# Attention and mixture block on one Trainium2 core: own PSUM banks for logits, maxima and job pieces, and a new order of TensorE's step

## The reference, cut to what matters

```python
h = _layernorm(x) * (1 + ca) + sa
# 16 heads of 16, causal, softmax over the keys with its exact maximum
logits = einsum('bhqd,bhkd->bhqk', q, k) / sqrt(16)
attn = softmax(where(causal, logits, -inf))
x = x + ga * (attn_times_v(attn, v) @ W_out.T + b_out)
h = _layernorm(x) * (1 + cb) + sb
# a layer: base product plus three low-rank experts of rank 8, mixed by softmax gates per token
h = relu(mole(h, W1, b1, A1, B1, R1))          # 256 -> 1024
x = x + gb * mole(h, W2, b2, A2, B2, R2)       # 1024 -> 256
```

## Time and profile before

| what | value |
|---|---|
| median of three runs | 1724.15 us |
| the profiled execution | 1730.61 us |
| its span (first to last instruction) | 1728.9 us |
| first exponential starts | 125.39 us |
| end of the last attention step, about | 1616 us |
| TensorE busy | 1412.8 us (82%) |
| DVE, ACT, POOL busy | 961.8, 685.5, 561.6 us |
| mean granted clock of TensorE | 0.808 |

### The profile page before, as it was taken

One profiled execution on the slowest core, in us unless ns is written; L12 is line 12 of the kernel. 1 busy time (PEld: TensorE's weight loads), 2 busy tenths in 40 slices (PEclk: granted clock), 3 DMA queues, 4 the chain that ended last, 5 costly groups with the idle time before them and its releaser, 6 DMA issues. The chain is left out here.

```text
span 1728.9 us, 26273 instructions
## 1 busy us (share of the span) xinstructions
PE 1412.8 (82%) x10096; PEld 796.4 (46%) x10096; DVE 961.8 (56%) x1878; ACT 685.5 (40%) x935; POOL 561.6 (32%) x680
## 2 busy tenths in 40 slices
PE   4458898897998989899857988889888889899445
PEld 4334454544544434454423554536453445454245
DVE  6146566566576676763336556665756667761212
ACT  1113354353443445355522433344533444546210
POOL 5460151324440124332302341234432233233262
PEclk8666588788996888888965786888995899899758
DMA  5242223121321121220241223113121112100000
GB/s 149 77 133 79 74 81 101 34 64 31 99 71 49 38 55 57 67 77 20 80 114 47 75 87 83 34 37 104 51 75 40 48 30 71 50 10 13 31 18 13
DMA packets 83638, 106.68 MB, mean 62 GB/s; under 512 B 9002, under 2 KB 57074, under 8 KB 83516
## 3 DMA queue, kind: packets, MB, share of 16 engines
q1 hardware_dynamic: 83516, 105.01, 21.5%
HBM read 66.71 MB, written 37.75 MB: 60 GB/s over the span
## 5 line engine op out<-in xcount | busy, mean ns | idle before, releaser
L853 DVE TENSOR_REDUCE mx<-ps 128x1 f32<-128x512 f32 (+3 forms) x1152 | 706.8, 655 | 436.7 <-PE ps L570 241.0
L759 ACT ACTIVATE prob<-ps 128x1024 f32<-128x1024 f32 (+3 forms) x640 | 567.1, 896 | 700.1 <-PE ps L548 368.6
L570 PE MATMUL ps<-kst,qst 48*128 48x512 f32 (+3 forms) x1280 | 321.7, 497 | 135.5 <-DVE mx L853 108.5
L607 PE MATMUL ps<-prob,vw 128*17 128x512 f32 (+3 forms) x2560 | 353.3, 630 | 1.6 <-ACT o_sb L766 0.9
L543 PE MATMUL ps<-qst,kst 50*128 50x512 f32 (+3 forms) x1280 | 333.4, 519 | 8.3 <-ACT prob L759 5.6
L543 PEld LDWEIGHTS ps<-qst,kst 50*128 50x128 f32 x1280 | 138.7, 213 | 331.7 <-issue 146.2
L570 PEld LDWEIGHTS ps<-kst,qst 48*128 48x128 f32 x1280 | 155.2, 226 | 213.6 <-issue 158.4
L1030 POOL CAST hid_hi<-hidf 128x512 fp32r<-128x512 f32 x64 | 39.1, 612 | 341.7 <-ACT hidf L810 341.6
L578 PE MATMUL ps<-mask_q,pick 64*128 64x128 bf16 x1024 | 88.6, 255 | 0.0
L707 PE MATMUL ps<-w_hi,hid_hi 128*128 128x284 f32 x256 | 81.5, 339 | 8.2 <-POOL hid_lo L1031 8.1
L607 PEld LDWEIGHTS ps<-prob,vw 128*17 128x17 f32 x2560 | 44.3, 99 | 88.8 <-issue 62.9
(11 more groups left out here) (147 smaller groups left out, 1801.5 us busy)
## 6 DMA issues: line engine op xcount, KB each, us to landing
kst<-k_rows SPq DMA_DIRECT2D x160, 192.0 KB, 4.0
qst<-q_rows SPq DMA_DIRECT2D x64, 192.0 KB, 3.9
q_rows<-s_hi SPq DMA_DIRECT2D x64, 128.0 KB
k_rows<-s_hi SPq DMA_DIRECT2D x64, 128.0 KB
o_rows<-o_sb SPq DMA_DIRECT2D x32, 256.0 KB, 2.0
sx<-in_x SPq DMA_DIRECT2D x16, 256.0 KB, 2.9
q_rows<-sf SPq DMA_DIRECT2D x32, 128.0 KB
k_rows<-sf SPq DMA_DIRECT2D x32, 128.0 KB
```

The lines of the kernel that those rows point to most:

```text
L570: last = pe.matmul(ps[:, M_BANK + banks[a], at:at + width], qst[half, u % Q_BUFS, p, i * P:(i + 1) * P], kst[half, K_SLOT[u, c], p, 0:widt ...
L607: last = pe.matmul(ps[32 * h:32 * h + HD + 1, O_BANK, skip:BLK], vw[:, (NJ * b + t // 4) % V_BUFS, t % 4, g * GH + h, :], prob[:, s % P_BU ...
L759: act.activation(prob[:, s % P_BUFS, 2 * p:2 * p + 2, 0:width], ps[:, bank:bank + 2, 0:width], ACT.Exp).then_inc(a_free, 1)
L853: dve.tensor_reduce(mx[:, u % 2, a, both, i, c], ps[:, M_BANK + bank, 0:n * width].rearrange("p (h x) -> p h x", h=n), AX, ALU.max).then_i ...
```

## The change

What it does, part by part:

- **Banks.** Logits get three single banks (0 to 2) in turn, one per head. Maxima and turned maxima get three banks (3 to 5). All job pieces share the single bank 6, in the order of the steps (`J_ORDER`; semaphores j_full, j_free). Bank 7 stays.
- **Exponentials** are taken per head (128 x 512): 1280 instructions instead of 640. A logits pair waits for the exponentials up to the first head of the pair before it.
- **TensorE's step** becomes `values(s - 2)`, `logits(s, 0)`, turn, first maxima, job piece, `logits(s, 1)`, second maxima.
- **Drains a step later.** ACT empties the job piece of step s in step s + 1, between the exponentials of heads 1 and 2; DVE does so between its two maxima groups; POOL at the start of step s + 1.
- **`place()`** hangs the pieces on steps, with at most one piece's matmuls in a step. In steps 0 to 319 there are 213 pieces on 239 steps (f_down takes two). Before, 159 steps hold one piece, 38 two, 3 three, and 120 none; now 81 hold none. 169 pieces are followed by another piece in the very next step: 109 of the earlier ones are drained by ACT, 60 by DVE.
- **Ends.** The token blocks sx are double-buffered (two loads up front); the first four S blocks and the last two F blocks have the norm and the splits on DVE instead of POOL; the weight split moves from POOL at step -8 to ACT and DVE at step -20; S blocks are stored in two halves, each after its own split.
- **Denominators** are inverted once per chunk (d_load, one reciprocal of 128 x 64, d_store), and the inverse is loaded by four DMAs with the attention output; before, each F block loaded them by six and DVE inverted 128 x 512 numbers (L908). fx has three buffers instead of two.

The diff, cut to its core:

```diff
-A_SLOTS, M_BANK, M_BANKS, O_BANK = 2, 4, 3, 7
+A_BANKS, M_BANK, M_BANKS, J_BANK, O_BANK = 3, 3, 3, 6, 7
...
+def place():
+    when, taken = {}, set()
+    for chain, starts in ((S_CHAIN, S_START), (D_CHAIN, D_START), (F_CHAIN, F_START)):
+        for n, start in enumerate(starts):
+            s = start
+            for piece, gap in chain:
+                s += gap
...
+                width = WIDTH.get(piece, 0)
+                while any(s + d in taken for d in range(width)):
+                    s += 1
+                when[piece, n] = s
+                taken.update(range(s, s + width))
+                s += max(0, width - 1)
...
 def logits(s, p):
-                    if event >= A_SLOTS:
-                        pe.wait_ge(a_free, event - A_SLOTS + 1)
+                    if event >= A_BANKS - 1:
+                        pe.wait_ge(a_free, event + 2 - A_BANKS)
...
+                def job_bank(piece, n):
+                    if J_AT[piece, n]:
+                        pe.wait_ge(j_free, J_AT[piece, n])
...
 TensorE's loop
                     first, second = groups(s)
+                    if 0 <= s - PV_LAG < NSTEP:
+                        values(s - PV_LAG)
                     if 0 <= s < NSTEP:
                         logits(s, 0)
                     if s in TURN_AT:
                         turn_maxima(TURN_AT[s])
                     for u, k in first:
                         maximum(u, k)
-                    if 0 <= s - PV_LAG < NSTEP:
-                        values(s - PV_LAG)
+                    for piece, n in JOBS[s]:
+                        if piece in pieces:
+                            pieces[piece](n)
                     if 0 <= s < NSTEP:
                         logits(s, 1)
                     for u, k in second:
                         maximum(u, k)
-                    for piece, n in JOBS[s]:
-                        if piece in pieces:
-                            pieces[piece](n)
...
 ACT's loop
                         exponential(s, 0)
                         exponential(s, 1)
+                    for piece, n in JOBS[s - 1]:
+                        if piece in drains:
+                            drains[piece](n)
+                    if 0 <= s < NSTEP:
+                        exponential(s, 2)
+                        exponential(s, 3)
...
 DVE's loop
-                    for u, k in first + second:
+                    for u, k in first:
                         maximum(u, k)
+                    for piece, n in JOBS[s - 1]:
+                        if piece in drains:
+                            drains[piece](n)
+                    for u, k in second:
+                        maximum(u, k)
```

More of the change, by code:

```diff
@@ L44 @@
 ST_ROWS = ROWS + 2
[L45 removed]
+K_BUFS, Q_BUFS, V_BUFS, P_BUFS, FX_BUFS = 7, 3, 6, 3, 3
 PV_LAG = 2
@@ L71, in job_steps @@
+WHEN = place()
+BEGIN, END = min(S_START) - 1, max(WHEN.values()) + 3
+def job_steps():
+    at = {s: [] for s in range(BEGIN - 1, END + 1)}
+    for (piece, n), s in WHEN.items():
+        if WIDTH.get(piece, 0) == 2:
+            at[s].append((piece + "a", n))
+            at[s + 1].append((piece + "b", n))
+        else:
+            at[s].append((piece, n))
     return at
 JOBS = job_steps()
+J_ORDER = sorted((s, piece, n) for (piece, n), s in WHEN.items() if piece in WIDTH)
+J_AT = {(piece, n): k for k, (_, piece, n) in enumerate(J_ORDER)}
@@ L91, in pair_steps @@
 def pair_steps():
-    at = {s: [] for s in range(BEGIN - 5, END)}
+    at = {s: [] for s in range(BEGIN - 1, END)}
     for u in range(NU):
@@ L132, in rings @@
             take(("max", u, k, 1))
-        if 0 <= s < NSTEP:
-            a_at["exp", s, 1] = len(a_at)
-        for piece, n in JOBS[s]:
[L136 to L146, removed]
+    return at
+M_AT = maxima_banks()
 def key_loads():
     blocks = [(u, c) for u, (_, J, _) in enumerate(UNITS) for c in range(J + 1)]
-    at = {s: [] for s in range(BEGIN - 5, END)}
+    at = {s: [] for s in range(BEGIN - 1, END)}
     for kb, (u, c) in enumerate(blocks):
@@ L436, in batch, with standardise, two_parts @@
             return n * TB // S
+        def standardise(eng, link, dst, src, mv, tmp, ready):
+            for t in range(TT):
+                last = eng.tensor_scalar(dst[:, t], src[:, t], mv[:, t, 0:1], tmp[:, 1, t:t + 1],
+                                         ALU.subtract, ALU.mult)
+                if t < TT - 1:
+                    link(last, wait=False)
+            last.then_inc(ready, 1)
+        def two_parts(eng, link, parts, src, ready):
+            link(eng.tensor_copy(parts[0], src))
+            eng.tensor_tensor(parts[1], src, parts[0].bitcast(F32), ALU.subtract).then_inc(ready, 1)
         with nc.Block() as block:
@@ L542, in logits @@
                         half = slice(64 * a, 64 * a + ST_ROWS)
-                        last = pe.matmul(ps[:, bank + a, 0:width], kst[half, slot, p, t % 4 * P:(t % 4 + 1) * P],
+                        last = pe.matmul(ps[:, banks[a], 0:width], kst[half, slot, p, t % 4 * P:(t % 4 + 1) * P],
                                          qst[half, u % Q_BUFS, p, skip:BLK], start=True, stop=(t < 4 * J))
@@ L547, in logits @@
                             half = slice(64 * a, 64 * a + 64)
-                            last = pe.matmul(ps[:, bank + a, 0:P], pick[half, w - a + 1], mask_k[half, w - a + 1],
+                            last = pe.matmul(ps[:, banks[a], 0:P], pick[half, w - a + 1], mask_k[half, w - a + 1],
                                              start=False, stop=(w == 1))
```

510 lines of the change are left out of this document (268 added, 242 removed).

## The result

The changed kernel takes 2053.32 us (median of four runs, 2043.85 to 2057.45); the kernel before, run beside it, 1728.22 us. The ratio is 1.188, 95% interval 1.180 to 1.196: slower by 19%. The prediction had the direction and the wait for the bank, but said 1831 us, in a range that ended at 1925.

The account below looks back on a forecast made before the run. The prediction took TensorE's own work to bound the kernel, 87% of the attention steps. Start -20, tail -6, bank wait +264 and removed waits -131 on 1728.9 gave a 1835.9 us span, 1831 us as time; range 1685 to 1925.

Parts of the forecast that it names:

- The wait for the bank: TensorE's job pieces that directly follow another wait for the single bank's late drain: 264 us, bounds nothing and 422.
- The waits that go: TensorE's waits for DVE's reduces and split maxima in the attention steps: 131 of 163 us go, bounds 55 and 163.
- The clock: TensorE's clock in the main stretch, left at the mean of before; could save at most 162 us or cost 90.
- the 0.05 that the text named as a sign of being wrong: The prediction is wrong if the clock of the main stretch moves by over 0.05.
- The case was among the rivals: Slower still: new gaps bring TensorE's lower clock in half of the upper-level steps, 1831 + 90 = 1921 us; chance 0.2.
- its 1.6 us a step: Growth of a job step's TensorE work and the bank wait's chain at the lower clock; 56 x 1.6 = 90 us.
- the one row of before with such a gap: At 1532.11, after a gap behind a reduce, two maxima matmuls take 0.79 us where the logits ahead took 0.50.
- the 70 that the text allowed for them: ACT's exponentials per head: up to 70 us if ACT's gaps were not there, otherwise no cost outside the bank's wait.
- The start: S block cycles before the first exponential get shorter: -20 us, bounds -10 and -29; first exponential near 105 us.
- the 13.7 worked out: Cycle between S blocks' drains at the start, 13.7 us instead of 23.2, with halves stored after their own splits.
- The tail: After the attention steps, denominators inverted once and splits on DVE: -6 us, bounds -14 and +2; about 107 us left.
- The sum: Whole kernel: 1728.9 - 20 - 6 + 264 - 131 = 1835.9 us span, 1831 us as the median time.

Follow-up runs that it names:

- the first run: Against the changed kernel, ACT and DVE empty a job piece in its own step instead of a step later: 1700.82 us, ratio to before 0.980.
- values back: Against the changed kernel, TensorE's values put back behind the first maxima group, bank and drains as changed: 1943.12 us, ratio to before 1.121.
- S turn later: Against the changed kernel with job pieces drained in their own step, twelve S blocks' loads, statistics and norm two steps earlier: 1636.03 us, ratio to before 0.9435.
- DVE's drains late: Against the 1636 us kernel (own-step drains, twelve S blocks' statistics two steps earlier), only DVE's drains a step later again: 1818.39 us, ratio 1.055.

## Why the prediction was right or wrong

- **The wait for the bank: right.** Worked out: 264 us, 1.56 on average. Measured: 235.6 us in 152 places, 1.55 each; ACT's part 135 for 153 (1.37 each for 1.40), DVE's 100 for 111 (1.89 for 1.85). The run with drains in their own step and the one with two banks take it to nothing, each by one half of its cause. The Trainium skill's rule on turning through banks ("Perfetto Trace Analysis", section "Optimizing Tensor Performance") fits the run with two banks; the first run shows that a single bank does as well here when its drain stands early in ACT's and DVE's programs.
- **The waits that go: too hopeful, and made up for by luck.** The prediction adds the 28.9 us of weight loads to the matmuls' waits of the earlier trace rows and gets 163; they stand in the same time, and 134.1 were there to be won. 131 were forecast, 85.4 went. Another 27.3 us of small waits went that the sum did not have; why they went was not looked at.
- **The clock: wrong, and the largest miss.** The step that failed is the clock "left at the mean of before, because it can go either way", at nothing in the sum. It fell from 0.83 to 0.76, 127 us of busy time, and the run with zeros shows that the new stands did it. The fall of 0.07 is beyond the 0.05 that the text named as a sign of being wrong. The case was among the rivals, at 1921 us and a chance of 0.2, with a price of 90 us. That price was too low: the text shows no working for its 1.6 us a step, and 3.57 us of work at 0.79 / 0.50 alone grow by 2.1. The chance was too small as well: the one row of before with such a gap pointed that way, and so did the Trainium skill's page "TensorE: Matmul & The Clock Gate", section "A second HAM failure mode: psum-queue depth-cycling", with which the run with zeros agrees (0.76 to 0.87).
- **Two waits not seen: 48 and 44 us.** `place()` puts the S turn one step behind the statistics (two before), while POOL needs a root and then a norm of 2.44 us in between; with three steps the wait is gone. The program's order showed that; I priced the moves of TensorE, not what each moved piece waits for. The 44 us of waits for exponentials lie inside the 70 that the text allowed for them, but at nothing in the sum. Values' part of them, 29.2 us in 23 places, belongs to the new order: it is 28.8 to 32.5 us in the runs that keep values ahead of the logits and 0.5 us in one place in both runs that put them back (0.6 before). For the logits' part, single exponentials and the ring of three banks were not tried apart, so which of them makes it is open.
- **The start: right in the cycles, wrong in what they hold up.** 20 us forecast, 7 measured. The three cycles of the S blocks took 25.1, 23.2 and 21.0 us; now they take 15.1, 19.0 and 16.2, together 19 us less. None is as short as the 13.7 worked out, but the sum counted two of the three. The store ends the wait of the second block's drain only; TensorE's products end the others. Before, then now:

```profile
40.67 0.84 ACT L786 ACTIVATE sf<-ps,bq_sb 128x256 f32<-128x256 f32 x2 [5.05 <-PE ps L616]
...
109.99 1.75 ACT L786 ACTIVATE sf<-ps,bq_sb 128x256 f32<-128x256 f32 x4 [11.14 <-DMA k_rows<-s_hi]
```

```profile
39.64 0.84 ACT L836 ACTIVATE sf<-ps,bq_sb 128x256 f32<-128x256 f32 x2 [4.21 <-PE ps L668]
...
54.73 0.84 ACT L836 ACTIVATE sf<-ps,bq_sb 128x256 f32<-128x256 f32 x2 [4.78 <-DMA k_rows<-s_hi]
...
73.77 0.84 ACT L836 ACTIVATE sf<-ps,bq_sb 128x256 f32<-128x256 f32 x2 [4.26 <-PE ps L668]
...
89.92 0.84 ACT L836 ACTIVATE sf<-ps,bq_sb 128x256 f32<-128x256 f32 x2 [4.26 <-PE ps L668]
...
118.36 1.08 ACT L804 ACTIVATE prob<-ps 128x512 f32<-128x512 f32 x2 [23.62 <-PE ps L602]
```

  The last block's drain starts 20 us earlier, but the first maxima start at the same time, before and now:

```profile
97.72 0.47 PE L570 MATMUL ps<-kst,qst 48*128 48x128 f32 x2
```

```profile
97.65 0.47 PE L624 MATMUL ps<-kst,qst 48*128 48x128 f32 x2
```

  Before, the products of the fourth S block stood between the maxima (steps -5 to -3, the maxima from -7 on). `place()` now puts them at steps -11 to -9, ahead of all maxima. So what the cycles won went into work that had run beside the maxima; that follows from the programs and these rows, and no run tried it apart.
- **The tail: right in size**, 6 us less (105.5 against 111.5, from the end of the last values). The terms of the text add up to -9.35 and it took -6; no run parts them.
- **The sum.** The attention steps were to grow by 133 us and grew by 341: 126.5 of the clock, 47.7 and 44.3 of the waits not seen, 45.6 of old waits that stayed, less 27.3 of others that went and 28.4 of bank waits that were smaller, is 208. With 13 us at the start that is 1831 + 208 + 13 = 2052 us.

## What to carry to other kernels

A single buffer between two engines cost nothing here where its drain stood early in the emptying engine's program, and a wait per use where it stood behind the next round's work: write down, for each buffer, what stands between the end of the filling and the start of the drain. A repeated stand of TensorE should be priced twice, once as the wait and once in the clock, here at two thirds of the idle time (145 us beside 213, all drains) to a little over it (97 beside 87, DVE's alone). When a planner moves pieces closer together, look at each piece's own inputs too, on every engine. And work that is done earlier helps only as far as what waits for it moves too: the last of the early S blocks was drained 20 us earlier, and the first exponential came 7 us earlier.

## What the runs showed that I had not expected

Adding 1216 matmuls of zeros in front of the job pieces made the kernel 117 us faster (2053 to 1936), with the granted clock of the attention steps at 0.87 instead of 0.76. And over the kernels here more idle time of TensorE in the attention steps mostly goes with a lower clock: 401 us at 0.76, 319 at 0.81 (values back), 189 at 0.84 (drains in their own step), 159 at 0.87 (S turn later). Not by the sum alone, though: 246 us (DVE's drains late) go with 0.81 and 235 (two banks) with 0.84, and the kernel before has 187 at 0.83. What else decides, perhaps where the stands lie, was not tried.
